# Gated cross-attention with a routed expert layer on one core: weight quarters, values and scores in another order

## The chip, the cores and the metric

The kernel runs on one core of one Trainium2 chip. The metric is device time in microseconds of one execution. Engines are called TensorE (PE), VectorE (DVE), ScalarE (ACT), GpSimd (POOL) and SyncE (SP); "queue" is an engine's stream of instructions, in which it also issues its transfers.

## The reference

Eight batches of 256 rows and 512 columns. Attention runs over the columns, with 16 heads of 16 channels; then every row is a token of a layer with 12 experts, of which it takes two.

```python
# x, ctx: (8, 256, 512);  Wq..Wo: (256, 256);  w1, w3: (12, 320, 512);  w2: (12, 512, 320)
h = layernorm(x)
q, k, v = Wq @ h + bq, Wk @ ctx + bk, Wv @ ctx + bv        # (256, 512) per batch, 16 heads x 16
p = softmax(q^T k / 4)                                     # (512, 512) per head
x = x + tanh(g0) * (Wo @ (p v) + bo)
h = layernorm(x)                                           # 2048 tokens of 512
w, i = top_k(softmax(h @ gate_w.T), 2);  w = w / sum(w)
x = x + tanh(g1) * sum over the two experts of w * ((silu(h @ w1.T) * (h @ w3.T)) @ w2.T)
```

## The kernel before

**Slots.** The attention runs as a pipeline of ten slots (`slots`, L351). In slot t, phase a projects batch t to K, Q and V, phase b makes scores, exponents and values of batch t-1, phase c normalises and projects the values of batch t-2 and makes its second layer norm and gate logits; p loads and normalises x and ctx of batch t+1. Slot 0 has only a and p, slot 1 has a, b and p, slot 8 has b and c, slot 9 only c. Slots 2 to 5 are a hardware loop of two rounds, the others are written out.

**Steps.** Each slot has 16 steps v (VS). In step v TensorE (L1327 to L1343) makes the first score group of step v+1 (`scores`, L1202: two heads of one quarter of the keys, into one of two PSUM tensors S), then the extra work that `EXTRA` (L322) lists for the step (k0, k1, q0, q1, v0 to v3 are projections into bank MA; o0, o1, t0, t1, lg are output projection, turning of the normed tokens and gate logits, in bank MC), then the second score group, then the values of step v (`values`, L1241). A score group waits until the exponent two groups earlier is made, since S has two tensors. ScalarE makes 32 exponents a slot (L724), two a step, of 1024 columns each. VectorE evicts MA, MC and O in the same order; every fourth step it copies O, the values and (in 16 rows of each 32) the sums of exponents, to `osum` (L982).

**Splits.** The experts' products are made with f16 high and low parts. The parts are made in 48 quarters of 512 KB in the shadow of the attention: ScalarE loads a quarter into one of three buffers wf (`load_quarter`, L697), VectorE writes high and low half to one of two buffers wp (`split_quarter`, L815: L823, L825), which first waits until the store of the quarter two before has landed, and ScalarE stores them (`store_quarter`, L702) and issues the load three quarters on. It does this in its own order, at the end of the exponents of the step two after the split, and waits there for the low half. `quarters` (L335) gives the steps: 4 quarters in slot 1, 6 in each of slots 2 to 7, 8 in slot 8. The experts' weights are read back after the last store.

**SyncE's order in a slot** (L435): loads for batch t+1; then for phase c a transfer of the sums (L461), their inverses to DRAM (L466), eight moves of 16 rows from `osum` to `oc` (L470), eight broadcasts of inverse sums to `zc` (L477); then for phase a the parts of K and Q go to DRAM in three copies each and are read back stacked (L482, L485); then the stores of x and of the normed tokens. Each waits where it stands, and what is behind it waits too.

**Phase c on VectorE.** At step ON_AT = 5 it multiplies `oc` by `zc` (L904) into `on` and casts to `os` (L906); GpSimd makes the low half (L580). LN_AT, XN_AT, XN2_AT and CS_AT are the steps of the layer norm's statistics, the norm, the second norm and the cast of the context.

**Experts.** After the attention the tokens are ranked and 43 tiles of 128 rows are gathered and run (`tiles`, L388).

A second version of the attention (`guard`) is there for inputs whose sums leave a range; it does not run here.

## Time and profile before

| | |
|---|---|
| median of 3 runs | 817.38 us (808.57 to 820.51) |
| profiled execution | 816.6 us, span 814.9 us |
| granted TensorE clock, mean | 0.88 |
| busy: TensorE / VectorE / ScalarE / GpSimd | 663.1 / 430.0 / 325.1 / 239.7 us |
| 16 DMA engines, mean over the span | 191 GB/s |

The granted clock is given as a share of 2.4 GHz; its other level is 1.2 GHz. Times in the rows count from the span's start. "[2.86 <-DVE V L931]" says that the engine stood idle for 2.86 us before the instruction, and that the V of line 931 on VectorE ended it. A row with "x4" is four instructions of one kind merged, with their time from first to last. "SPq" and "ACTq" are transfers issued by those queues; their time is that of the issue.

### The profile page before, as it was taken

The page shows a single profiled execution, that of the slowest core. Times are in us where ns is not written, and L with a number is a line of the kernel's source. Part 1 is how long each engine was busy: PE and PEld are TensorE (multiplying, and loading weights), DVE is VectorE, ACT ScalarE, POOL GpSimd, SP SyncE. Part 2 cuts the span into 40 slices and gives each one's busy share as a digit, 9 for nine tenths or more (in the row PEclk, how much of TensorE's full clock was granted, in tenths as well). Part 3 has the DMA queues.
Part 4 walks back from the last instruction along what each step waited for, and adds up shares of the span by engine and source line. Part 5 has one row for each costly group of instructions (what it writes and reads, how often), then busy time and mean ns, then how long its engine had stood idle before and what let it go on. Part 6 is the DMA issues. An engine that isn't in the chain of part 4 may idle for free.

```text
span 814.9 us, 14231 instructions
## 1 busy us (share of the span) xinstructions
PE 663.1 (81%) x4335; PEld 303.2 (37%) x4336; DVE 430.0 (53%) x761; ACT 325.1 (40%) x391; POOL 239.7 (29%) x184
## 2 busy tenths in 40 slices
PE   5878976977979879879876825059999999999993
PEld 3712222312222223232221113046666666666661
DVE  5536667585794785665646743753333333333330
ACT  0047855745646556546555610002222222222221
POOL 4032223222331331322111102233354433454422
PEclk8879989998997989879888865569999999999998
DMA  8447877768787887857767537524677787664533
GB/s 249 139 129 241 258 247 247 220 224 277 199 276 200 254 267 215 265 163 200 244 208 207 182 106 259 205 81 92 169 185 212 230 222 205 182 116 91 84 47 39
DMA packets 68470, 155.56 MB, mean 191 GB/s; under 512 B 9733, under 2 KB 15366, under 8 KB 66886
## 3 DMA queue, kind: packets, MB, share of 16 engines
q1 hardware_dynamic: 36368, 76.56, 29.8%
q10 hardware_dynamic: 22422, 55.87, 21.0%
q0 software_dynamic: 9632, 22.55, 14.6%
q8 instruction: 22, 0.36, 0.2%
q14 instruction: 26, 0.21, 0.1%
HBM read 92.04 MB, written 58.46 MB: 185 GB/s over the span
## 4 chain that ended last, share of the span: by engine, by line
PE 49%; DVE 15%; DMA 12%; issue 9%; SPq 8%; POOL 2%; ACT 2%; ACTq 2%; DVEq 0%; POOLq 0%
PE S L1393 15%; PE O L1414 9%; PE O L1253 7%; DMA ocz<-inverse_sums 5%; PE S L1214 5%; SPq L470 4%; DMA out<-yo,slot_out 3%; SPq L477 3%; DVE wp L825 3%; PE MC L1288 3%; PE MA L1288 2%; PE S L1380 2%; ACT prob L724 2%; PE MC L1308 2%; DVE wp L823 2%
## 5 line engine op out<-in xcount | busy, mean ns | idle before, releaser
L724 ACT ACTIVATE prob<-S 128x1024 f32<-128x1024 f32 x256 | 253.2, 1025 | 207.8 <-PE S L1214 144.0
L1253 PE MATMUL O<-prob,V 128*32 128x512 f32 x1024 | 156.0, 685 | 0.1
L1393 PE MATMUL S<-W,xT 128*128 x1032 | 149.9, 303 | 1.2 <-DVE xT L1158 1.2
L1214 PE MATMUL S<-Q,K 48*128 48x512 f16 x512 | 107.9, 428 | 52.2 <-ACT prob L724 46.0
L1393 PEld LDWEIGHTS S<-W,xT 128*128 128x128 f16 x1032 | 100.2, 99 | 39.0 <-issue 1.4
L1214 PEld LDWEIGHTS S<-Q,K 48*128 48x128 f16 x512 | 24.4, 94 | 216.9 <-ACT prob L724 149.7
L652 POOL DMA_INDIRECT out<-yo,slot_out x43 | 69.0, 1604 | 119.8 <-ACT yo L769 71.7
L1414 PE MATMUL O<-W,hT 128*128 (+1 forms) x344 | 90.3, 381 | 1.0 <-DVE hT L1178 1.0
L1166 DVE SCALAR_TENSOR_TENSOR hh<-S,act 128x320 f32<-128x320 f32 x43 | 21.1, 492 | 126.9 <-PE S L1393 124.2
L825 DVE SCALAR_TENSOR_TENSOR wp<-wf,wp 128x1024 f16<-128x1024 f32 x48 | 82.4, 1716 | 1.7
L628 POOL DMA_INDIRECT xg<-tokens_normed,slot_tok x43 | 42.6, 990 | 44.7 <-PE S L1380 32.5
L769 ACT ACTIVATE yo<-O,slot_w 128x512 f32<-128x512 f32 x43 | 29.6, 688 | 60.7 <-PE O L1414 56.4
L763 ACT ACTIVATE hs<-hh 128x320 f16<-128x320 f32 x43 | 20.2, 470 | 78.2 <-DVE hh L1166 78.2
L756 ACT ACTIVATE act<-S 128x320 f32<-128x320 f32 x43 | 18.8, 437 | 79.3 <-PE S L1393 75.8
L1414 PEld LDWEIGHTS O<-W,hT 128*128 128x128 f16 (+1 forms) x344 | 31.6, 97 | 49.4 <-issue 29.1
L1270 PE MATMUL MA<-w4s,cs 128*128 128x256 f16 x192 | 29.7, 296 | 22.4 <-DVE V L931 20.3
L823 DVE TENSOR_SCALAR wp<-wf 128x1024 f16<-128x1024 f32 x48 | 47.7, 993 | 0.1
L580 POOL TENSOR_TENSOR ks<-kf,ks 128x1024 f16<-128x1024 f32 x7 | 14.9, 2134 | 110.8 <-DVE ks L924 110.8
L580 POOL TENSOR_TENSOR os<-kf,os 128x1024 f16<-128x1024 f32 x8 | 17.4, 2171 | 94.5 <-DVE os L906 94.5
L1288 PE MATMUL MC<-os,w4s 128*128 128x512 f16 x96 | 32.9, 477 | 14.3 <-DVE os L906 12.1
L982 DVE COPY osum<-O 128x512 f32<-128x512 f32 x32 | 22.0, 687 | 40.5 <-PE O L1253 40.5
L1178 DVE COPY hT<-S 128x640 f16<-128x640 f16 x43 | 21.2, 492 | 41.3 <-PE S L1404 40.3
(152 smaller groups left out, 670.7 us busy)
## 6 DMA issues: line engine op xcount, KB each, us to landing
wf<-wall ACTq DMA_DIRECT2D x48, 512.0 KB, 6.7
weight_parts<-wp ACTq DMA_DIRECT2D x48, 512.0 KB, 4.7
W<-weight_parts SPq DMA_DIRECT2D x10, 2048.0 KB, 9.7
K<-k_parts SPq DMA_DIRECT2D x8, 1024.0 KB, 6.7
Q<-q_parts SPq DMA_DIRECT2D x8, 1024.0 KB, 6.7
k_parts<-ks SPq DMA_DIRECT2D x24, 256.0 KB
q_parts<-qs SPq DMA_DIRECT2D x24, 256.0 KB
ctx<-ctx_in SPq DMA_DIRECT2D x8, 512.0 KB, 6.0
```

What stands on the lines that cost most here:

```text
L470: sp.dma_start(oc[dst0:dst0 + DK, :, :], src).then_inc(g.oz, 16)
L580: pool.tensor_tensor(parts[:, 1], f[:, :, :], parts[:, 0], ALU.subtract).then_inc(lo, 1)
L628: pool.indirect_dma_start(out=xg[j % TR][:, :], out_offset=None, in_=xn_dram[:, :], in_offset=bass.IndirectOffsetOnAxis(ap=slot_tok[:, j:j ...
L652: pool.indirect_dma_start(out=out[:, :], out_offset=bass.IndirectOffsetOnAxis(ap=slot_out[:, j:j + 1], axis=0), in_=yo[j % TR][:, :], in_o ...
L724: act.activation(prob[:, u % RING, :], S[u % 2][:, :], ACT.Exp, scale=SCALE).then_inc(g.exp, 1)
L823: dve.tensor_scalar(c[:, 0], w[:, :], WS, None, ALU.mult).then_inc(s_whi, 1)
L825: dve.scalar_tensor_tensor(out=c[:, 1], in0=w[:, :], scalar=WS, in1=c[:, 0], op0=ALU.mult, op1=ALU.subtract).then_inc(s_wlo, 1)
L1214: last = pe.matmul(S[u % 2][:, s * T:(s + 1) * T], K[par][r0:r0 + rows_, 2 * g4 + n, st * P:(st + 1) * P], Q[par][r0:r0 + rows_, 2 * g4 + ...
L1253: last = pe.matmul(O[g4 % 2][2 * DK * j:2 * DK * (j + 1), :], V[par][:, st, head(g4, j), :], prob[:, u % RING, (j % 2) * T:(j % 2 + 1) * T ...
L1288: last = pe.matmul(bank[:, :], w4s[:, wp_, w, k, m * P:(m + 1) * P], src[:, xp, k, :], start=(n == 0), stop=(n == 3 * CT - 1))
L1393: last = pe.matmul(ps, xT[par][:, xp * TT + k, :], W[:, bass.ds(off + (w * WCOL + (2 * k + n) * F), F)], start=(k == 0 and (xp, w) == (0, 0)),
L1414: last = pe.matmul(y_ps[:, :], hT[par][0:rows_, block, :], W[0:rows_, bass.ds(off + (w * WCOL + W2 + k * T), T)], start=(n == 0), stop=(n ...
```

## The change

- Weights: four quarters in each of slots 2 to 7 (steps 2, 6, 9, 12), four at the end of slot 0, eight in slots 1 and 8, two in slot 9, two in the first two expert tiles. Four buffers wf instead of three. SyncE stores the quarters, in places of its own order between the transfers of K and Q; ScalarE only issues the load four quarters on, at the exponents of the step three after the split. In slot 0 it does so ahead of its first exponent. The read of the last expert's weights waits for the last stores, the others do not.
- Values: `osum` holds the groups in another order, so that four moves bring the second half of the values over the rows that held the sums, once these are read. The multiply reads `osum` itself. The inverse sums come in one broadcast. The rows of Wo are laid out to match. The low half of the normed values is made by VectorE, not GpSimd. `xn2` shares its memory with `xn`, with waits for that.
- SyncE's order: phase c's transfers and K's writes come first, then the loads for batch t+1.
- Scores: both score groups of step v+1 come ahead of the step's extra work. o0 and o1 move to steps 8 and 9 (o1 no longer in two halves), t0, t1, lg to 13, 14, 15.

```diff
-    WFS = 3
+    WFS = 4
-    z_dram = nc.dram_tensor("inverse_sums", [GH, GROUPS, T], F32).ap()
+    z_dram = nc.dram_tensor("inverse_sums", [GH, 2, CT * T], F32).ap()
-        xn2 = sb("xn2", [P, CT, T], F32, att)
+        xn2 = xn
-        EXTRA = {0: "k0", 1: "k1", 2: "q0", 3: "q1", 4: "v0", 5: "v1", 6: "v2", 7: "o0", 8: "o1a", 9: "o1b",
-                 10: "v3", 12: "t0", 13: "t1", 14: "lg"}
-        ON_AT, LN_AT, XN_AT, XN2_AT, CS_AT, SPLIT_AT = 5, 6, 8, 10, 11, 3
-        OZ = 16 * 4 * GH
+        EXTRA = {0: "k0", 1: "k1", 2: "q0", 3: "q1", 4: "v0", 5: "v1", 6: "v2", 8: "o0", 9: "o1",
+                 10: "v3", 13: "t0", 14: "t1", 15: "lg"}
+        ON_AT, LN_AT, XN_AT, XN2_AT, CS_AT, SPLIT_AT = 5, 7, 8, 11, 12, 3
+        OZ = 16 * (GH + 1)
@@ quarters
-            if t.i is None and t.add in (0, B + 1):
-                return []
-            if t.i is None and t.add == 1:
-                steps, first = (4, 7, 10, 13), At(None, 0, 0)
+            if t.i is None and t.add == 0:
+                steps, first = (15, 15, 15, 15), At(None, 0, 0)
+            elif t.i is None and t.add == 1:
+                steps, first = (1, 3, 5, 7, 9, 11, 13, 14), At(None, 0, 4)
             elif t.i is None and t.add == B:
-                steps, first = (0, 2, 4, 6, 8, 10, 12, 13), At(None, 0, QUARTERS - 8)
+                steps, first = (0, 2, 4, 6, 8, 10, 12, 13), At(None, 0, QUARTERS - 12)
+            elif t.i is None and t.add == B + 1:
+                steps, first = (7, 7), At(None, 0, QUARTERS - 4)
             else:
-                steps = (0, 2, 5, 8, 10, 13)
-                first = At(t.i, 12, 4 + 6 * (t.add - 2)) if t.i is not None else At(None, 0, 4 + 6 * (t.add - 2))
+                steps, first = (2, 6, 9, 12), At(t.i, 4 * t.mul, 4 * t.add + 4)
@@ SyncE, one slot
+                    def over_sums(j):
+                        r0 = 2 * DK * j
+                        sp.dma_start(osum[par][r0 + DK:r0 + 2 * DK, 0:CT, :], osum[par][r0:r0 + DK, CT:2 * CT, :])\
+                            .then_inc(g.oz, 16)
+                    if c:
+                        bc = t.before(2)
+                        wait(sp, g.os, bc, GROUPS, GROUPS, s_bog)
+                        wait(sp, g.on, bc, 1, 1)
+                        sp.dma_start(zl[:, :], osum[par][DK::2 * DK, :, :]).then_inc(g.zl, 16)
+                        wait(sp, g.rz, bc, 1, 1)
+                        sp.dma_start(z_dram.rearrange("j h n -> (j h n)").rearrange("(p n) -> p n", p=P), zr[:, :]).then_inc(g.zst, 16)
+                        for j in range(GH):
+                            over_sums(j)
+                    if a:
+                        wait(sp, g.qk, t, KQ_READS, 0, s_bog)
+                        wait(sp, g.kh, t, 1, 1)
+                        write(k_dram, ks, 0, (0, 1), g.kst)
+                    if c:
+                        wait(sp, g.zst, bc, 16, 16)
+                        sp.dma_start(zc.rearrange("p m t -> p (m t)"),
+                                     z_dram.rearrange("j h n -> (j h) n").unsqueeze(1)
+                                     .to_broadcast([2 * GH, DK, CT * T])).then_inc(g.oz, 16)
+                    if a:
+                        wait(sp, g.kl, t, 1, 1)
+                        write(k_dram, ks, 1, (2,), g.kst)
                     if p:
...
                         load_ctx(nxt)
                         load_x(nxt)
...
                     if a:
+                        weights(0, 3)
                         wait(sp, g.qh, t, 1, 1, s_bog)
                         write(q_dram, qs, 0, (0, 2), g.qst)
...
                         read(K, k_dram)
                         wait(sp, g.ql, t, 1, 1, s_bog)
                         write(q_dram, qs, 1, (1,), g.qst)
                         wait(sp, g.qst, t, KQ_WRITES, KQ_WRITES, s_bog)
                         read(Q, q_dram)
+                        weights(3, 10)
+                    else:
+                        weights(0, 9)
...
+                    weights(10 if a else 9, VS)
@@ ScalarE
-            def store_quarter(q):
-                c = q.add % 4
-                wait(act, s_wlo, q, 1, 1, s_bias)
-                act.dma_start(w_dram[bass.ds(over(q, 4).value(), 1), :, :, c * WQ:(c + 1) * WQ]
-                              .rearrange("e p h n -> p (e h) n"), wp[q.add % 2][:, :, :]).then_inc(s_wst[q.add % 2], 16)
+            def load_behind(q):
                 if q.i is not None or q.add + WFS < QUARTERS:
+                    wait(act, s_wlo, q, 1, 1, s_bias)
                     load_quarter(q.before(-WFS))
...
                     if not b_:
+                        if a and not guard:
+                            for n in range(WFS):
+                                load_quarter(At(None, 0, n))
+                        for _, q in splits:
+                            load_behind(q)
                         return
...
-                            if u == 2 * min(v + 2, VS - 1) + 1:
-                                store_quarter(q)
+                            if u == 2 * min(v + 3, VS - 1) + 1:
+                                load_behind(q)
@@ VectorE
-                            dve.tensor_tensor(on[:, :, :], oc[:, :, :], zc[:, :, :], ALU.mult).then_inc(g.on, 1)
+                            dve.tensor_tensor(on[:, :, :], osum[par][:, 0:CT, :], zc[:, :, :], ALU.mult)\
+                                .then_inc(g.on, 1)
                             wait(dve, g.on, bc, 1, 2)
                             dve.tensor_copy(os_[:, 0], on[:, :, :]).then_inc(g.oh, 1)
+                            low(bc, os_, on, g.oh, g.ol)
...
-                            dve.tensor_copy(osum[1 - par][:, g4, :], O[g4 % 2][:, :]).then_inc(g.os, 1)
+                            at = g4 % 2 * CT + g4 // 2
+                            dve.tensor_copy(osum[1 - par][:, at, :], O[g4 % 2][:, :]).then_inc(g.os, 1)
@@ TensorE
                     for v in range(VS):
                         if b_ and v + 1 < VS:
-                            scores(bb, 1 - par, v + 1, (0,))
+                            scores(bb, 1 - par, v + 1)
                         what = EXTRA.get(v, "")
...
-                        if b_ and v + 1 < VS:
-                            scores(bb, 1 - par, v + 1, (1,))
```

## Rows read from the trace of the kernel before

**Rows 1.** windows by slot: stretch, length, busy us per engine, clock, DMA share, GB/s

```profile
46.10:90.10 44.00, 40.18 (x244) 10.18 (x242) 20.95 (x30) 32.69 (x34) 9.56 (x7) 0.89 0.65 209
...
90.10:146.90 56.80, 45.37 (x279) 13.94 (x278) 39.04 (x55) 31.74 (x33) 15.42 (x10) 0.91 0.76 239
...
257.30:312.40 55.10, 47.31 (x277) 14.12 (x278) 38.08 (x54) 31.65 (x32) 15.39 (x10) 0.87 0.77 243
...
424.90:473.90 49.00, 37.40 (x224) 9.15 (x220) 30.52 (x39) 29.08 (x30) 5.94 (x4) 0.86 0.58 183
...
473.90:515.00 41.10, 11.99 (x38) 6.72 (x38) 15.29 (x74) 0.56 (x2) 5.17 (x4) 0.53 0.50 164
...
542.00:815.00 273.00, 257.72 (x1927) 163.18 (x1927) 89.28 (x214) 68.59 (x129) 107.40 (x82) 0.98 0.60 142
```

**Rows 2.** timeline of slot 5, first half: start, us, engine, operation, [idle]

```profile
261.97 0.35 SPq L466 DMA_DIRECT2D inverse_sums<-zr  x1
...
265.90 4.03 SPq L477 DMA_DIRECT2D ocz<-inverse_sums  x8
...
270.11 1.97 SPq L482 DMA_DIRECT2D k_parts<-ks  x3
...
274.92 1.23 DVE L904 TENSOR_TENSOR kf<-ocz 128x1024 f32<-128x1024 f32 x1 [4.10 <-DMA ocz<-inverse_sums]
...
277.26 0.83 PE L1270 MATMUL MA<-w4s,cs 128*128 128x256 f16 x6 [2.86 <-DVE V L931]
```

**Rows 3.** timeline of slot 5, second half, same columns

```profile
292.75 0.39 PE L1214 MATMUL S<-Q,K 48*128 48x512 f16 x2 [1.58 <-ACT prob L724]
...
295.76 3.02 DVE L825 SCALAR_TENSOR_TENSOR wp<-wf,wp 128x1024 f16<-128x1024 f32 x1
...
299.01 0.56 ACTq L706 DMA_DIRECT2D weight_parts<-wp  x1
...
301.63 0.39 PE L1214 MATMUL S<-Q,K 48*128 48x512 f16 x2 [2.82 <-ACT prob L724]
```

**Rows 4.** page, part 5: groups of instructions, busy us and mean ns, idle before

```profile
L724 ACT ACTIVATE prob<-S 128x1024 f32<-128x1024 f32 x256 | 253.2, 1025 | 207.8 <-PE S L1214 144.0
...
L1166 DVE SCALAR_TENSOR_TENSOR hh<-S,act 128x320 f32<-128x320 f32 x43 | 21.1, 492 | 126.9 <-PE S L1393 124.2
...
L825 DVE SCALAR_TENSOR_TENSOR wp<-wf,wp 128x1024 f16<-128x1024 f32 x48 | 82.4, 1716 | 1.7
...
L823 DVE TENSOR_SCALAR wp<-wf 128x1024 f16<-128x1024 f32 x48 | 47.7, 993 | 0.1
```

**Rows 5.** page, part 6: issues of the context's load, KB each, us to landing

```profile
ctx<-ctx_in SPq DMA_DIRECT2D x8, 512.0 KB, 6.0
```

**Rows 6.** timeline, end of slot 0

```profile
41.50 2.50 DVE L848 CAST cs<-ctx 128x1024 f16<-128x1024 f32 x1
...
46.08 2.85 ACT L724 ACTIVATE prob<-S 128x1024 f32<-128x1024 f32 x3 [34.34 <-PE S L1214]
```

**Rows 7.** stores of the weights, line 706: issue to landing

```profile
DMA to landing us min/median/max: 3.1/4.7/8.8
```

**Rows 8.** timeline of slot 1: SyncE's queue and ScalarE

```profile
64.92 1.15 SPq L482 DMA_DIRECT2D q_parts<-qs  x1
...
75.40 0.37 SPq L485 DMA_DIRECT2D Q<-q_parts  x1
...
75.48 2.85 ACT L724 ACTIVATE prob<-S 128x1024 f32<-128x1024 f32 x3 [1.67 <-PE O L1253]
```

**Rows 9.** reads of Q: issue to landing

```profile
DMA to landing us min/median/max: 5.4/6.7/10.0
```

**Rows 10.** timeline, last slot

```profile
481.07 3.85 SPq L477 DMA_DIRECT2D ocz<-inverse_sums  x8
...
486.83 1.23 DVE L904 TENSOR_TENSOR kf<-ocz 128x1024 f32<-128x1024 f32 x1 [4.54 <-issue]
```

**Rows 11.** windows of slot 5, its last stretch

```profile
303.00:312.40 9.40, 9.40 (x54) 3.09 (x54) 3.11 (x5) 5.41 (x6) 0.00 (x0) 0.69 0.76 254
```

90 lines of the change are left out of this document (44 added, 46 removed).

## The prediction

> **What bounds the kernel now.** I cut the span into stages first [rows 1], by the starts of the slots. Slot 1 takes 44.0 us, slots 2 to 7 together 334.8 us (from 90.1 to 424.9, so 55.8 each), slot 8 takes 49.0, the last slot and what follows it 41.1, and the expert tiles 273.0. In the tiles TensorE is busy for 257.7 of 273 us at a granted clock of 0.98; the change hardly touches them. So the question is the slots.
>
> Take slot 5 as the pattern, in the third row of [rows 1]: 55.10 us, TensorE busy 47.31 at a mean granted clock of 0.87. 47.31 x 0.87 = 41.2 us is the work at full clock, 6.1 us is what the lower clock costs, and 55.10 - 47.31 = 7.8 us TensorE stands idle. ScalarE is busy 31.7, VectorE 38.1. No engine but TensorE is near the slot's length, so a slot can fall only by the idle time and by the clock that is lost behind it.
>
> The timeline names the idle pieces. First, step 5: VectorE waits 4.10 us for the last of the inverse sums, the values' multiply comes at 274.92, the eviction of the values' projection is queued behind it, and TensorE stands 2.86 us [rows 2]. Its next products run on the low clock. Second and third, [rows 3]: ScalarE holds its queue until a quarter's low half is written, then issues a store and a load; TensorE waits 1.58 and then 2.82 us for the exponent behind it. The low half before the longer wait took 3.02 us, against a mean of 1.72 [rows 4]: it lies beside GpSimd's own subtraction of the same kind of tile. The three make 7.26 of the 7.8 us; the rest, 0.5, I count to the second wait.
>
> **The change, part by part.** The sum is made against the profiled execution, 816.6 us, which is 0.8 below the median of the runs.
>
> *Fewer quarters in slots 2 to 7, stores on SyncE, load waits a step later.* Two of six splits go from each slot. A split is 0.99 + 1.72 = 2.7 us of VectorE [rows 4], 5.4 us a slot. ScalarE now waits at the steps' ends 3 behind the split instead of 2, and issues one transfer instead of two (0.56 us for the store by [rows 3]; I take 0.6 for each). The waits of 2.1 and 2.82 us go: 4.9 us a slot. What is late next is VectorE itself in steps 9 to 13: residual and statistics, a split, the second layer norm, copy of sums, context cast, another split that lies beside GpSimd's subtractions (up to 3.7), and only then the eviction of the first turned tile, for which TensorE waits before it turns the second. Counting these from the rows' durations gives about 11.3 us from the end of "o1" to that eviction, where TensorE needs some 10. I put 2.0 us of new idle there, between 0 and 4.
>
> *Values moved in place, inverse sums in one broadcast.* Before, SyncE issued four moves, the store of the inverse sums at 261.97, four more moves and, from 265.90, 8 broadcasts (4.03), the last of which let VectorE go at 274.92; the writes of K stood behind them until 270.11 [rows 2]. Now 4 moves come behind the store of the inverse sums, two K writes (0.66 each, from 1.97 for three) and one broadcast of 512 KB. Counted from the slot's start at 257.3: the store at +4.7 [rows 2], moves until +8 (the last four took about 3.5 before the first broadcast), K writes until +9.5, the broadcast issued by +10. A 512 KB load of this queue lands after 6.0 us [rows 5], so at +16 against +17.6 now; with the moves and K writes ahead of it on the queue up to +18. Against this, the low half of the values moves from GpSimd to VectorE, ahead of the eviction that TensorE waits for: as long as the multiply of the same size, 1.23 us [rows 2]. So the 2.86 us become about 2.0 (between 0 and 6). GpSimd's 2.1 us are free, which costs nothing: it had slack (15.4 busy of 55.1).
>
> *Both score groups first.* In the projection steps TensorE runs without a gap in either order, so nothing. In other steps it helps ScalarE a little; below 0.5 us a slot, taken as 0. It may also cost: the projection now stands behind the second group, which needs the exponent before. It is covered while ScalarE (two exponents of 1.03 a step [rows 4]) is ahead of TensorE, which it is once its waits are gone.
>
> Slots 2 to 7: idle 7.8 becomes 2.0 + 2.0 = 4.0, so -3.8; with less of it, the clock's loss of 6.1 falls perhaps by its share to 4.3, so -1.8. Together -5.6 a slot, **-33.6** for six. Ends: no gain, and -9 a slot (all idle but 1 us gone and half of the clock's loss).
>
> *Slot 0, four splits at its end.* This costs. There are two buffers of split quarters, so the third split waits until the first store landed and the fourth for the second. SyncE issues these only after the read of Q. VectorE is free at 44.0 (41.50 + 2.50, [rows 6]). Split one lies beside GpSimd's subtraction for the context: 3.0 for the low half as in [rows 3] and 0.7 for the high one, to 47.7. Split two is undisturbed, 0.7 + 1.23 as the multiply of [rows 2], so 1.95 with what lies between, to 49.7. Store one is issued at 47.8 and lands 4.7 us later [rows 7], 52.5; split three to 54.5; store two landed by then; split four to 56.5. ScalarE has all four waits for them in its queue ahead of the first exponent, and issues a load (0.6). So the first exponent starts near 57 instead of 46.08 [rows 6]: **+11**. With landings of 3.1 us it is +9, with 8.8 us +15 [rows 7]. Nothing covers it: TensorE's scores of the batch were there when ScalarE began, and both engines had been waiting.
>
> *Slot 1, eight splits instead of four.* The store of the split at step 3 stands in SyncE's order behind the read of Q. That read was issued 29.3 us after the first exponent (75.40 against 46.08), since the write of Q's low half, issued at 64.92 behind the 1 MB read of K, took 10.5 us [rows 8]. The read of Q lands after 5.4 to 10.0 us [rows 9], the store behind it, say 8 us after its issue: +37.5. Only then can VectorE make the split of step 7, whose end, +39.5, is what ScalarE's queue waits for after its 22nd exponent; it had done that one at +31 [rows 8], and would now at +33. That is 6 to 7 us. Four more splits, each waiting for a store of 4.7 us two before it, add some 3 at the slot's end: **+10**, between +2 and +14.
>
> Here a rule speaks against my term, after the row: the 10.5 us show transfers of one queue staying behind each other. The Trainium skill (DMA: Bandwidth & Descriptors, "Issuing engines are not separate DMA queues") says that transfers of all issuing engines run on the same 16 engines and interleave, and that issuing from several saves only issue time. By that the store would take its 4.7 us wherever it is issued, slot 1's term would be about +6 and the whole 4 us less. The trace does not show a store behind a 1 MB read on one queue, so it leaves this open; the issue order behind SyncE's wait would stay in either case.
>
> *Slot 8.* No projections; the broadcast follows the moves at once, about 4 us earlier, and ScalarE's store issues go. But the split of step 13 waits for the store of step 10, which stands behind the tokens' store, perhaps 3 us. 49.0 becomes 46: **-3** (-7 to +1).
>
> *Last slot.* The eight broadcasts from 481.07 took 3.85 us and the multiply came at 486.83 [rows 10]; one issue and 5 to 6 us of landing make that 1 us earlier (0 to 2). The low half saves 0.9 more. Two splits at step 7 (1.95 each, with GpSimd idle) stand ahead of the first residual and cost 2. **0** (-2 to +3). The last two splits lie in the gap of 124.2 / 42 = 2.96 us in which VectorE waits in each tile [rows 4]: **+0.5** (0 to 2).
>
> Sum: 11 + 10 - 33.6 - 3 + 0 + 0.5 = -15.1; 816.6 - 15.1 = 801.5, so 802.
>
> **The rivals.** *Slots fall further.* With no wait at the turned tiles and the broadcast landing at +15, TensorE would hold its clock: -8.5 a slot, -51, with the start at +19: 778 to 785. For it: GpSimd and ScalarE have slack (15.4 and 31.7 busy of 55.1 [rows 1]). Against it: VectorE's chain in steps 9 to 13 is as long as TensorE's. Chance 0.25.
>
> *Half the gain.* The chain through steps 9 to 13 costs 4 us and the clock gives nothing back: -3 a slot, -18; start +21: about 817, no change. For it: the clock was at 0.69 from 303.0 to 312.4, though TensorE was busy for all of that stretch [rows 11]. Chance 0.2.
>
> *Slower: the broadcast is late.* It stands behind moves and K writes on one queue and is one transfer, not eight in flight. If it lands at +20 instead of +17.6, the multiply, and 1.23 us of the low half on top, hold the projection at step 6 for 2.86 + 2.4 + 1.2 = 6.5 us. With 2.0 at the turned tiles that is 8.5 of idle, as much as before; the slots gain nothing, and the start's 21 less slot 8's 3 stand: 835. It decides from a landing at about +20 on. For it: 5.0 us passed between the end of the eight issues and the multiply [rows 2]. Against: 4 moves and 7 issues are gone from ahead of it. Chance 0.1.
>
> *The change does not do what it says* in one part: reordering the scores. It moves no number above.
>
> **How the numbers follow.** My forecast, 790 to 813, has 0.45. A difference under 2% (801 to 834) is about what a measurement of this kernel cannot tell from none. The forecast's half below 801 (0.21) and the first rival (0.25) are faster: 0.46. The other half (0.24) and the second rival (0.2) are the same: 0.44. Slower: 0.10. The range, 779 to 827, leaves out the far end of the first rival and the slower one.
>
> **What would show it.** First exponent near 57 us (right: 55 to 61). In slot 1, one stall of ScalarE of 5 to 9 us before its 23rd exponent. Slots 2 to 7 at 50 us, with splits in four steps, no ScalarE idle over 3 us, TensorE's largest idle at step 6 and at the second turned tile. The multiply 16 to 18 us into the slot. If the first exponent starts before 50, or slots stay above 54, the forecast is wrong.

## The result and the profile after

The change makes the kernel slower: 844.14 us (843.04 to 845.38, 4 runs) against 814.65 (4 runs of the kernel before), ratio 1.036, 95% interval 1.028 to 1.045. The profiled execution has a span of 842.9 us at a mean granted clock of 0.861, against 814.9 and 0.880: 28.0 us to explain. By 2% the verdict is "slower", where I forecast 802.

Windows by slot answer to [rows 1]: stretch, length, busy us per engine, clock, DMA share, GB/s. The second row is slots 2 to 7 together, the third slot 5, the fourth slot 8.

```profile
58.60:119.40 60.80, 40.35 (x240) 9.57 (x240) 31.23 (x38) 30.54 (x32) 10.21 (x6) 0.81 0.67 214
119.40:446.50 327.10, 274.93 (x1658) 86.14 (x1658) 196.76 (x293) 186.19 (x194) 80.17 (x50) 0.86 0.65 202
288.20:343.90 55.70, 46.80 (x278) 15.08 (x280) 33.83 (x51) 31.60 (x33) 14.33 (x9) 0.84 0.63 194
446.50:499.20 52.70, 36.28 (x224) 10.69 (x222) 29.62 (x40) 28.98 (x31) 3.06 (x3) 0.88 0.69 197
```

The same window over slots 2 to 7 of the kernel before:

```profile
89.90:424.80 334.90, 279.96 (x1658) 85.40 (x1659) 224.01 (x311) 191.61 (x193) 86.87 (x56) 0.88 0.75 233
```

So slots 2 to 7 are 7.8 us shorter (7.7 between the copies of sums that end them), not 33.6. Length is idle time plus busy time, and busy time times clock is the work: before, per slot, 9.2 idle, 41.1 work and 5.6 lost to the clock; after, 8.7 idle, 39.4 work and 6.4 lost to the clock (the clock is rounded to 0.01, so each of the last two terms is good to 0.2 us a slot). TensorE waits nearly as long as before and runs no faster. The work fell by 1.7 us though the number of products is the same; the run f3 below shows that the order of the products alone moves time between "busy" and "idle", so the two terms are compared with care between kernels of different order. Slot 1 is 60.8 against 43.9, slot 8 52.7 against 49.2, and the first exponent comes 12.5 us later.

Slot 5, first half, answers to [rows 2]; columns are start, us, engine, operation, count, and in brackets the idle time before it with its releaser:

```profile
292.13 0.36 SPq L484 DMA_DIRECT2D inverse_sums<-zr  x1
292.52 2.53 SPq L466 DMA_DIRECT2D osum<-osum  x4
295.39 1.35 SPq L471 DMA_DIRECT2D k_parts<-ks  x2
296.85 0.63 SPq L496 DMA_DIRECT2D ocz<-inverse_sums  x1
...
306.18 1.23 DVE L938 TENSOR_TENSOR kf<-osum,ocz 128x1024 f32<-128x1024 f32 x1 [3.78 <-DMA ocz<-inverse_sums]
...
309.31 0.42 DVE L967 SCALAR_TENSOR_TENSOR V<-MA,bv_all 128x256 f32<-128x256 f32 x1
...
309.79 1.46 PE L1313 MATMUL MA<-w4s,cs 128*128 128x256 f16 x6 [4.01 <-DVE V L967]
```

Counted from the copy of sums that ends the slot before (288.22 here, 256.81 in the kernel before), the one broadcast is issued at +8.6, where the eight had begun at +9.1. The multiply comes 9.33 us after that issue, against 9.02 before, so at +18.0 against +18.1; then the low half and the eviction, and TensorE has stood 4.01 us where it had stood 2.86.

Slot 5, second half, answers to [rows 3]:

```profile
327.81 2.24 DVE L880 CAST cs<-ctx 128x1024 f16<-128x1024 f32 x1
329.98 0.68 DVE L855 TENSOR_SCALAR wp<-wf 128x1024 f16<-128x1024 f32 x1
330.69 3.03 DVE L857 SCALAR_TENSOR_TENSOR wp<-wf,wp 128x1024 f16<-128x1024 f32 x1
333.64 0.68 DVE L987 COPY xT<-MC 128x512 f32<-128x512 f32 x1
...
334.45 1.11 PE L1347 MATMUL MC<-ident,xn 128*128 128x128 f32 x4 [3.71 <-DVE xT L987]
...
337.36 3.59 PE L1351 MATMUL MC<-gate,xT 128*128 128x12 f32 x16
...
341.53 1.94 ACT L747 ACTIVATE prob<-S 128x1024 f32<-128x1024 f32 x2 [8.95 <-PE S L1257]
```

VectorE takes the context's cast (2.24) and the split (0.68 + 3.03) ahead of the first turned tile's copy at 333.64. TensorE waits 3.71 for it. Then the gate's product takes 3.59 us, and ScalarE has nothing to do for 8.95 us, since the scores for it stand behind that product. The two waits of [rows 3] on ScalarE's store are gone; this one took their place.

The waits of TensorE over slots 2 to 7 (total us, times, longest), first of the changed kernel, then of the kernel before:

```profile
PE MA L1313 <- DVE V L967: 25.4, 6, 4.9
PE MC L1347 <- DVE xT L987: 19.4, 6, 3.7
PE S L1257 <- ACT prob L747: 9.9, 11, 5.0
```

```profile
PE S L1214 <- ACT prob L724: 34.5, 17, 4.4
PE MA L1270 <- DVE V L931: 20.3, 6, 4.6
```

The wait for exponents fell by 24.6 us, the wait at step 6 grew by 5.1, and 19.4 us for the turned tile are new. The changed kernel's lines of groups and of DMA issues that bear on the rest:

```profile
L747 ACT ACTIVATE prob<-S 128x1024 f32<-128x1024 f32 x256 | 245.7, 1023 | 229.3 <-PE S L1257 158.4
...
L855 DVE TENSOR_SCALAR wp<-wf 128x1024 f16<-128x1024 f32 x48 | 37.8, 787 | 38.1 <-DMA weight_parts<-wp 37.8
...
weight_parts<-wp SPq DMA_DIRECT2D x46, 512.0 KB, 6.9
...
ctx<-ctx_in SPq DMA_DIRECT2D x8, 512.0 KB, 10.4
```

The start, answering to [rows 6] and [rows 8], and slot 8:

```profile
44.58 3.02 DVE L857 SCALAR_TENSOR_TENSOR wp<-wf,wp 128x1024 f16<-128x1024 f32 x1
...
47.63 11.09 SPq L427 DMA_DIRECT2D weight_parts<-wp  x4
...
53.67 0.69 DVE L855 TENSOR_SCALAR wp<-wf 128x1024 f16<-128x1024 f32 x1 [4.21 <-DMA weight_parts<-wp]
...
58.57 1.94 ACT L747 ACTIVATE prob<-S 128x1024 f32<-128x1024 f32 x2 [46.62 <-DVE wp L857]
...
93.22 0.37 SPq L474 DMA_DIRECT2D Q<-q_parts  x1
...
100.67 0.69 DVE L855 TENSOR_SCALAR wp<-wf 128x1024 f16<-128x1024 f32 x1 [12.17 <-DMA weight_parts<-wp]
...
103.09 3.77 ACT L747 ACTIVATE prob<-S 128x1024 f32<-128x1024 f32 x4 [11.50 <-DVE wp L857]
...
454.56 0.64 SPq L496 DMA_DIRECT2D ocz<-inverse_sums  x1
455.25 17.27 SPq L427 DMA_DIRECT2D weight_parts<-wp  x4
...
465.03 0.69 DVE L855 TENSOR_SCALAR wp<-wf 128x1024 f16<-128x1024 f32 x1 [10.03 <-DMA weight_parts<-wp]
...
466.90 1.22 DVE L938 TENSOR_TENSOR kf<-osum,ocz 128x1024 f32<-128x1024 f32 x1
```

The first exponent waits for four splits. In slot 1 SyncE reads Q at 93.22; the store behind it lets VectorE go at 100.67 after 12.17 us, and ScalarE, which waits for that split, stands 11.50 us. In slot 8 the store is issued at 455.25, right behind the broadcast, and VectorE waits 10.03 us for it. The multiply stands behind that split in VectorE's order; by slot 5's 9.33 us from issue to multiply the inverse sums would be there at 463.9, three microseconds before it starts; that is an estimate, since in slot 8 of e5 below the same span was 10.25. Of the 37.8 us that VectorE waits for stores, 22.7 lie in slots 0 and 1, 15.1 behind slot 7, and none between.

### The profile page after: what moved, and what is told of

Its sections match the earlier page's. It is cut to its first block, busy times and chain, and to the rows that moved or that the text cites. A ratio compares the mean times of both kernels' runs of the same rounds, so it can differ in the third digit from the quotient of the medians.

```text
span 842.9 us, 14098 instructions
## 1 busy us (share of the span) xinstructions
PE 657.0 (78%) x4335; PEld 305.1 (36%) x4336; DVE 429.9 (51%) x769; ACT 317.6 (38%) x391; POOL 229.0 (27%) x176
## 4 chain that ended last, share of the span: by engine, by line
PE 46%; DMA 20%; DVE 16%; issue 9%; POOL 3%; SPq 2%; PEldq 1%; ACT 1%; POOLq 0%; DVEq 0%; ACTq 0%
PE S L1434 15%; PE O L1455 8%; DMA weight_parts<-wp 6%; DMA ocz<-inverse_sums 6%; PE O L1296 6%; PE MA L1331 4%; DMA out<-yo,slot_out 3%; PE MC L1351 3%; PE S L1257 3%; DMA q_parts<-qs 3%; DVE wp L857 2%; PE MC L1331 2%; PE S L1421 2%; DVE wp L855 2%; POOL rstd L612 1%
## 5 line engine op out<-in xcount | busy, mean ns | idle before, releaser
L747 ACT ACTIVATE prob<-S 128x1024 f32<-128x1024 f32 x256 | 245.7, 1023 | 229.3 <-PE S L1257 158.4
L1257 PE MATMUL S<-Q,K 48*128 48x512 f16 x512 | 92.9, 422 | 51.6 <-ACT prob L747 43.7
L1434 PEld LDWEIGHTS S<-W,xT 128*128 128x128 f16 x1032 | 99.9, 98 | 38.5 <-issue 1.4
L1257 PEld LDWEIGHTS S<-Q,K 48*128 48x128 f16 x512 | 19.8, 95 | 180.4 <-ACT prob L747 150.8
L857 DVE SCALAR_TENSOR_TENSOR wp<-wf,wp 128x1024 f16<-128x1024 f32 x48 | 73.2, 1526 | 1.7
L610 POOL TENSOR_SCALAR veps<-mv 128x2 f32<-128x2 f32 x16 | 6.2, 385 | 197.7 <-DVE mv L997 101.6
L855 DVE TENSOR_SCALAR wp<-wf 128x1024 f16<-128x1024 f32 x48 | 37.8, 787 | 38.1 <-DMA weight_parts<-wp 37.8
L652 POOL DMA_INDIRECT xg<-tokens_normed,slot_tok x43 | 42.4, 987 | 42.6 <-PE S L1421 30.1
L1296 PEld LDWEIGHTS O<-prob,V 128*32 128x32 f32 x1024 | 21.1, 113 | 46.6 <-issue 34.2
L1331 PE MATMUL MC<-os,w4s 128*128 128x512 f16 x96 | 27.3, 427 | 13.6 <-DVE os L941 10.7
## 6 DMA issues: line engine op xcount, KB each, us to landing
ctx<-ctx_in SPq DMA_DIRECT2D x8, 512.0 KB, 10.4
```

What stands on the lines that cost most here:

```text
L652: pool.indirect_dma_start(out=xg[j % TR][:, :], out_offset=None, in_=xn_dram[:, :], in_offset=bass.IndirectOffsetOnAxis(ap=slot_tok[:, j:j ...
L747: act.activation(prob[:, u % RING, :], S[u % 2][:, :], ACT.Exp, scale=SCALE).then_inc(g.exp, 1)
L855: dve.tensor_scalar(c[:, 0], w[:, :], WS, None, ALU.mult).then_inc(s_whi, 1)
L857: dve.scalar_tensor_tensor(out=c[:, 1], in0=w[:, :], scalar=WS, in1=c[:, 0], op0=ALU.mult, op1=ALU.subtract).then_inc(s_wlo, 1)
L1257: last = pe.matmul(S[u % 2][:, s * T:(s + 1) * T], K[par][r0:r0 + rows_, 2 * g4 + n, st * P:(st + 1) * P], Q[par][r0:r0 + rows_, 2 * g4 + ...
L1296: last = pe.matmul(O[g4 % 2][2 * DK * j:2 * DK * (j + 1), :], V[par][:, st, head(g4, j), :], prob[:, u % RING, (j % 2) * T:(j % 2 + 1) * T ...
```

## The experiments

They are told by question. The edits are shown shortened: words in angle brackets stand for code that is left out, and so are semaphore counts that go with an edit. This table has the profiled execution of each, in us: the first exponent, the length of slot 1, of slots 2 to 7 together, of slot 8, and of all behind it. A slot ends where its fourth copy of sums starts, as in the windows above. Each length is of one execution: the profiled ones lie up to 9.5 us from the median of their kernel (g2 847.48 against 838.00, e1 828.60 against 835.48, f4 779.87 against 786.38), and stretches that an edit doesn't touch differ by up to 4 us. So a difference of a few microseconds in a stretch says nothing by itself. Ratios are to runs of the kernel before on the same chip, with a 95% interval.

| kernel | first exp. | slot 1 | 2 to 7 | slot 8 | rest | ratio |
|---|---|---|---|---|---|---|
| before | 46.1 | 43.9 | 334.8 | 49.2 | 341.0 | 1 |
| after | 58.6 | 60.8 | 327.1 | 52.7 | 343.7 | 1.036 [1.028, 1.045] |
| i1 split at 14 | 58.8 | 60.8 | 295.1 | 55.2 | 342.8 | 0.991 [0.988, 0.994] |
| e5 ScalarE stores | 59.2 | 48.8 | 327.8 | 42.9 | 343.4 | 0.999 [0.995, 1.003] |
| e1 eight pieces | 58.9 | 60.8 | 311.5 | 54.1 | 341.1 | 1.020 [1.010, 1.029] |
| e3 multiply at 7 | 59.9 | 60.9 | 318.6 | 53.6 | 342.8 | 1.027 [1.020, 1.034] |
| e4 old quarters | 46.4 | 48.8 | 359.2 | 52.2 | 340.2 | 1.035 [1.027, 1.044] |
| g2 store first | 60.1 | 55.3 | 331.3 | 55.5 | 343.3 | 1.024 [1.015, 1.032] |
| g3 two halves | 60.4 | 47.6 | 322.6 | 42.4 | 340.9 | 1.002 [0.998, 1.006] |
| f1 next scores | 60.8 | 48.4 | 318.9 | 41.9 | 343.8 | 1.007 [0.997, 1.016] |
| f3 order alone | 48.3 | 43.9 | 333.3 | 52.4 | 340.5 | 1.012 [1.000, 1.024] |
| f2 e5 + e1 | 60.0 | 49.2 | 303.1 | 43.3 | 341.4 | 0.987 [0.978, 0.995] |
| h1 f2 + multiply at 7 | 59.3 | 49.2 | 306.7 | 43.8 | 342.7 | 0.983 [0.976, 0.990] |
| h2 f2 + split at 14 | 59.7 | 47.8 | 283.6 | 45.9 | 342.4 | 0.956 [0.949, 0.962] |
| h3 f2 + next scores | 59.9 | 47.6 | 305.9 | 42.4 | 341.5 | 0.984 [0.976, 0.993] |
| f4 f2 + all three | 60.1 | 47.7 | 287.2 | 41.7 | 341.4 | 0.967 [0.956, 0.979] |
| g1 f4, two splits first | 51.8 | 47.7 | 288.2 | 41.5 | 343.2 | 0.954 [0.946, 0.962] |
| h4 g1, SyncE stores | 50.7 | 62.1 | 286.5 | 56.5 | 345.4 | 0.977 [0.969, 0.984] |
| g5 g1, later loads | 46.6 | 48.7 | 290.3 | 42.6 | 342.7 | 0.950 [0.942, 0.958] |
| i2 | 47.8 | 50.0 | 283.5 | 42.2 | 343.9 | 0.938 [0.933, 0.944] |

My theories after the result: (A) the stores in SyncE's queue cost the start, slot 8 and perhaps the slots; (B) the single broadcast is slow; (C) the order of the last steps costs the slots. Rival to each: what it costs is covered, or moves elsewhere.

### Where the stores are issued

**e5, the stores on ScalarE again,** all else as changed:

```diff
-    (SyncE) for v, q in splits: if v0 <= v < v1: store_quarter(q)
+    (ScalarE, load_behind) wait(act, s_wlo, q, 1, 1, s_bias); act.dma_start(<store of q>)
```

> The changed kernel with its own schedule of quarters, but each store issued by ScalarE ahead of the load behind it, none by SyncE. Theory A: the stores' place in SyncE's order, behind the read of Q, is what holds VectorE for 12.2 us in slot 1, and the queue's order behind the broadcast what holds it for 10.0 in slot 8: both waits fall below 4 us, slot 0 stays as it is (first exponent near 58), slots 2 to 7 keep their length within 1.5 us; total 818 to 830. Rival B: stores are slow wherever they are issued: slot 1 stays above 56 us, total within 5 us of 844.

822.80 us; 1.036 becomes 0.999. Slot 1 falls by 12.0 us and slot 8 by 9.8, slots 2 to 7 do not move. The stores land 4.4 us after their issue instead of 6.9. So the place of the stores costs the two slots in which a split follows closely on a store, and there alone.

**g2, in slot 1 the store of step 3's quarter ahead of the wait for Q's parts and the read of Q:**

```diff
+    if t.i is None and t.add == 1: weights(3, 5)
     wait(sp, g.qst, t, KQ_WRITES, KQ_WRITES, s_bog); read(Q, q_dram)
-    weights(3, 10)
+    weights(5 if t.i is None and t.add == 1 else 3, 10)
```

> The changed kernel with, in slot 1 alone, the store of step 3's quarter ahead of SyncE's wait for Q's low half and the read of Q. Theory A (the predicted one): it is SyncE's order, the store standing behind that wait, that holds VectorE for 12.2 us at step 7; the wait falls under 4 us and slot 1 from 60.8 to 48 to 53 us, total 8 to 12 us less. Rival B: the transfers of one queue stay behind each other in any case, so the store and with it Q land as late: slot 1 stays above 57.

838.00 us. Slot 1 is 55.3, between the 60.8 of the change and the 48.8 of e5. VectorE's wait at this split:

```profile
94.90 0.69 DVE L857 TENSOR_SCALAR wp<-wf 128x1024 f16<-128x1024 f32 x1 [4.92 <-DMA weight_parts<-wp]
```

against 12.17. So the order behind Q's read is worth some 5.5 of slot 1's 12 us. The trace of the changed kernel agrees: of the 12.17 us, from 88.50 on, 5.1 had passed when SyncE issued the first store behind Q's read at 93.64, and 7.0 lie between that issue and the landing. What is left in g2 are waits for later stores, 2.73, 2.96 and 2.03 us, which still stand in SyncE's order. Slot 8 is untouched by this edit and did not gain (55.5).

**h4, the kernel g1 (below) with the stores by SyncE:**

```diff
-    (ScalarE, load_behind) act.dma_start(<store of q>)
+    (SyncE) for v, q in splits: if v0 <= v < v1: store_quarter(q)
```

> The kernel of g1 (two splits in slot 0, eight-piece broadcast, multiply at step 7, split at step 14, next scores first), with the stores issued by SyncE again in place of ScalarE. If SyncE's queue is the cause by itself, slot 1 is over 55 us (47.7), slot 8 over 50 (41.5), and the ratio is 0.97 to 0.99 (g1: 0.954). Rival: it was slow only through the broadcast in the same queue: slot 8 under 44, ratio under 0.96.

801.98 us. The first theory holds on both slots (62.1 and 56.5), though the broadcast here is eight pieces: stores issued by SyncE, with their place in its order, cost 14.4 + 15.0 us, and slots 2 to 7 nothing (286.5 against 288.2). In slot 8 of it:

```profile
418.76 0.69 DVE L856 TENSOR_SCALAR wp<-wf 128x1024 f16<-128x1024 f32 x1 [9.13 <-DMA weight_parts<-wp]
```

The store that it waits for was issued at 412.69, behind the eight pieces: 3.1 us of this wait lie before the issue and 6.1 behind it.

**e4, quarters, steps and counts of splits as before,** six a slot and none in slot 0, all else as changed:

```diff
-    steps, first = (2, 6, 9, 12), At(t.i, 4 * t.mul, 4 * t.add + 4)
+    steps, first = (0, 2, 5, 8, 10, 13), At(t.i, 12, 4 + 6 * (t.add - 2))   # and four, not eight, in slot 1
```

> The changed kernel with the quarters at the steps of the kernel before (none in slot 0, 4 in slot 1, 6 in slots 2 to 7, 8 in slot 8), stores still by SyncE, four load buffers. Theory A: slots 0 and 1 end near 92 us instead of 119.4, since no split waits for a store there; slots 2 to 7 grow by 1 to 3 us each for two more splits: total 822 to 835. Rival B: the start costs nothing that the other slots don't give back, and the order of SyncE's queue with more stores in it is the cause: 840 or more.

848.92 us, as slow as the change, but elsewhere: the first exponent is back at 46.4 and slot 1 at 48.8, while slots 2 to 7 take 359.2. The multiply comes 19.4 to 23.1 us into a slot. Six splits a slot, with all else as changed, take 24.4 us more over these slots than before the change; whether by the stores, the broadcast or the steps, this run doesn't separate. It shows that the longer start alone is not the cause of the loss, and that fewer splits a slot were a part of the change that helped.

### The broadcast

**e1, the broadcast in eight pieces,** as before the change but with values in place:

```diff
-    sp.dma_start(zc, z_dram.rearrange("j h n -> (j h) n").unsqueeze(1).to_broadcast([2 * GH, DK, CT * T]))
+    for r in range(2 * GH):
+        sp.dma_start(zc[DK * r:DK * (r + 1)], z_dram[r // 2, r % 2:r % 2 + 1, :].to_broadcast([DK, CT * T]))
```

> The changed kernel with its one broadcast of inverse sums (512 KB) issued as eight of 64 KB, all else equal. Theory A: the single broadcast is slow by itself and holds what stands behind it on SyncE's queue (9.3 us to the multiply in slot 5, 7.0 in the last slot where nothing competes, and VectorE's 10.0 us wait for a store in slot 8). Then the multiply of the last slot comes about 6 us after the first broadcast's issue instead of 7, in slots 2 to 7 it comes 15 to 16.5 us after the slot's start instead of 18, slot 8's wait falls to about 5 us, and the total falls by 8 to 18 us, to 826 to 836. Rival B: the queue is late because of the weights' stores that now stand in it; then the multiply stays within 1 us of where it was, and the total within 5 us of 844.

835.48 us, 1.036 becomes 1.020. In the profiled execution the slots gain 15.6 us; it was the fastest of four, and the ratios give some 14 us for the whole kernel. Its slot 5 begins at 278 us; the eight issues and the multiply:

```profile
286.50 4.61 SPq L497 DMA_DIRECT2D ocz<-inverse_sums  x8
...
293.41 1.23 DVE L939 TENSOR_TENSOR kf<-osum,ocz 128x1024 f32<-128x1024 f32 x1 [1.36 <-DMA ocz<-inverse_sums]
```

6.91 us from the first issue to the multiply instead of 9.33, though the issues alone take 4.61. The single broadcast saves SyncE 4 us of issuing and costs 2.4 us where it counts. Before the change eight pieces took 9.02 us [rows 2]: eight moves were ahead of them, four of them issued right before, where now there are four moves in all. That this is the reason isn't shown.

**f2, the edits of e1 and e5 together:**

> The kernel with the stores by ScalarE, and the broadcast of inverse sums in eight pieces. Theory A: the broadcast is slow by itself, so its 14 us add to the stores' 30: 0.978 to 0.988 of before, the multiply 15 to 17 us into the slots. Rival B: the broadcast was slow only since it shared a queue with the stores: 0.995 to 1.003.

801.64 us, faster than before the change (0.987). With the stores on ScalarE the eight pieces are worth 24.7 us over the slots (327.8 to 303.1).

**g3, e5 with the broadcast in two halves of columns,** each from the same eight rows:

```diff
-    sp.dma_start(zc, <all columns>)
+    for m in range(CT): sp.dma_start(zc[:, m, :], <columns m * T to (m + 1) * T>)
```

> The kernel with the stores by ScalarE, and the broadcast as two transfers, each of all 128 rows and half the columns. In the last slot the single one needed 7.0 us from issue to multiply at no more than 185 GB/s, where the eight pieces reached up to 287. Theory A: the eight source rows as the outermost dimension keep the transfer to half of the DMA engines; two halves have the same eight rows and so stay at 185 GB/s and 7 us, and the total stays within 4 us of the run with one. Rival B: one transfer is slow because it is one; two overlap, the multiply comes 1 us or more earlier and the total falls by 8 us or more, as with eight.

816.23 us, 1.002, as e5 within the intervals. The slots have 5.2 us less. In the last slot the multiply comes 6.06 us after the first issue; for the one broadcast it was 6.95 (505.93 to 512.88) and for the eight before it 5.76 [rows 10]. So the number of transfers may help a little. Windows of one microsecond in the last slot, of the changed kernel and then of e1, show how the two ways move:

```profile
508.60:509.60 1.00, 0.00 (x0) 0.00 (x0) 0.00 (x0) 0.00 (x0) 0.00 (x0) 0.50 0.52 131
509.60:510.60 1.00, 0.00 (x0) 0.00 (x0) 0.00 (x0) 0.00 (x0) 0.00 (x0) 0.50 0.54 131
```

```profile
495.00:496.00 1.00, 0.00 (x0) 0.00 (x0) 0.00 (x0) 0.00 (x0) 0.00 (x0) 0.50 0.62 131
496.00:497.00 1.00, 0.00 (x0) 0.00 (x0) 0.00 (x0) 0.00 (x0) 0.00 (x0) 0.50 0.74 127
```

The single broadcast keeps about half of the DMA engines' time busy, as the expectation's first theory had it, but it moves as many bytes as the eight pieces, 131 GB/s; the 185 and 287 GB/s that the expectation names don't show in these windows. So why one broadcast of 512 KB is slower than eight of 64 KB is not settled: no run changed the number of source rows.

**e3, the multiply at step 7 instead of 5:**

```diff
-        ON_AT, LN_AT, XN_AT, XN2_AT, CS_AT, SPLIT_AT = 5, 7, 8, 11, 12, 3
+        ON_AT, LN_AT, XN_AT, XN2_AT, CS_AT, SPLIT_AT = 7, 7, 8, 11, 12, 3
```

> The changed kernel with the multiply by the inverse sums at step 7 instead of 5, all else equal, so that no eviction of a values' projection stands behind the wait for the broadcast. Theory A: TensorE's 4.2 us a slot of waiting at step 6, and the low clock behind it, are a loss of their own: slots 2 to 7 fall by 4 to 5 us each, the total to 815 to 822. Rival B: what is gained at step 6 is lost again at the turned tiles in steps 13 to 14, where VectorE is late anyway: less than 10 us in total, 835 or more.

842.52 us, as the changed kernel within the intervals (1.027 against 1.036). Its profiled execution, the fastest of four, has 8.5 us less in the slots. The wait at step 6 is gone, but the wait for the turned tile grew from 19.4 to 37.1 us over the six slots: the time saved at step 6 went largely there, as the rival had it.

**h1, the same edit on f2:**

> The kernel with the eight-piece broadcast and the stores on ScalarE (slots 2 to 7: 303.1 us), with the values' multiply issued in step 7 in place of step 5. If the wait at the multiply still costs there, it gives 1.5 to 3 us a slot, sum 285 to 294. Rival: the broadcast in eight pieces lands in time and the multiply in step 5 costs nothing; then the later multiply only makes the copies behind it later: sum 300 or more.

804.67 us, slots 306.7: the rival holds. Once the multiply comes at +15.4 to +16.9, as in slots 3 to 7 of f2, there is no more to gain here.

### The last steps of a slot

**f4, f2 with three edits,** the multiply at step 7, the fourth split at step 14, and the next slot's scores ahead of the logits:

```diff
-    ON_AT = 5;  steps = (2, 6, 9, 12)
+    ON_AT = 7;  steps = (2, 6, 9, 14)
+    if b_ and v == VS - 1 and not last_b and not guard: scores(t, par, 0)   # ahead of EXTRA
     what = EXTRA.get(v, "")
```

> All mends together: stores by ScalarE, broadcast in eight pieces, multiply at step 7, next batch's scores ahead of the logits, and the split of step 12 at step 14, behind the evictions of the turned tiles. Theory A: each wait is its own loss, so they add: slots 2 to 7 near 47 to 49 us, 0.935 to 0.955 of before, with slots 0 and 1 still at 105 to 110 us. Rival B: VectorE's chain of steps 9 to 14 takes over: slots above 51 us, 0.965 or more.

786.38 us, slots 287.2. What f2 left in the slots is in one of the three; h1, h2 and h3 take them one by one.

**h2, f2 with the fourth split at step 14:**

```diff
-                steps, first = (2, 6, 9, 12), At(t.i, 4 * t.mul, 4 * t.add + 4)
+                steps, first = (2, 6, 9, 14), At(t.i, 4 * t.mul, 4 * t.add + 4)
```

> The same kernel with only the fourth split moved from step 12 to step 14, behind the turned tiles' copies. If the split holds those copies up (the wait of PE for xT), it gives 1 to 3 us a slot, sum 285 to 297, and the xT wait of 3.7 us a slot falls under 1.5. Rival: the wait only moves to the logits: sum 301 or more.

781.63 us, slots 283.6, a little below the 285 to 297 of the first theory: the whole gain of f4 by one number, 19.5 us of f2's slots or 3.3 a slot. The wait for the turned tile is 1.4 us in all instead of 16.4.

**h3, f2 with the last of f4's edits alone,** the next slot's scores ahead of the logits:

> The same kernel with only the next slot's scores issued ahead of the logits at the end of a slot. With the stores still as they were this gave 8.9 us over six slots (327.8 to 318.9). If the terms add: sum 294. Rival: it hides the same idle time that the earlier broadcast already took: sum 300 or more.

804.40 us, slots 305.9: nothing; the rival holds. **f1**, the same edit on e5:

> The kernel with the stores by ScalarE (the fourth experiment), and in step 15 the next batch's first scores ahead of the gate logits instead of behind them. Theory A: since the logits were moved to the last step, which has no score group of its own ahead of them, ScalarE stands 7.9 us there in each slot (323 to 331 us of slot 5), and TensorE's low clock makes it dear; with the scores first slots 2 to 7 fall by 2 to 3.5 us each, the total to 0.97 to 0.985 of before. Rival B: TensorE is the bound at the slot's end, whatever the order: the sum of slots 2 to 7 stays within 4 us of 327.8 and the total at 0.995 to 1.003.

816.93 us. Here the slots of the profiled execution fell by 8.9 us, but the ratio is 1.007, against 0.999 for e5 in another set of runs: the timed runs show no gain of this edit.

**i1, the split at step 14 as the only edit of the changed kernel:**

> The changed kernel with one number altered: the fourth split in step 14 in place of 12. If the split ahead of the turned tiles' copies is a loss of its own, slots 2 to 7 fall from 327.1 us by 12 to 20 us, to 307 to 315, and the ratio from 1.036 to about 1.015. Rival: while the stores and the single broadcast are late, the time only moves to the wait at step 6: sum 320 or more.

812.08 us: 1.036 becomes 0.991, and slots 2 to 7 fall by 32.0 us to 295.1, more than either theory had. The other single edits of the changed kernel give 15.6 us at most in the slots. Its window over slots 2 to 7, then the copies of the turned tiles, the split behind them, the gate's product and ScalarE's wait in its slot 5:

```profile
119.50:414.60 295.10, 255.02 (x1658) 78.20 (x1658) 187.06 (x293) 185.70 (x194) 78.33 (x50) 0.93 0.71 221
```

```profile
311.93 0.68 DVE L987 COPY xT<-MC 128x512 f32<-128x512 f32 x1
...
314.32 1.96 PE L1351 MATMUL MC<-gate,xT 128*128 128x12 f32 x16
...
314.81 1.22 DVE L857 SCALAR_TENSOR_TENSOR wp<-wf,wp 128x1024 f16<-128x1024 f32 x1
...
316.82 3.77 ACT L747 ACTIVATE prob<-S 128x1024 f32<-128x1024 f32 x4 [2.30 <-PE S L1257]
```

The copy of the first turned tile follows the context's cast at once and TensorE doesn't wait. The split's low half, no longer beside GpSimd's subtraction (330.14 to 332.64 in the changed kernel's slot 5), takes 1.22 us instead of 3.03; the gate's product 1.96 instead of 3.59; ScalarE stands 2.30 instead of 8.95. By the windows the six slots have 12.1 us less idle time of TensorE (52.2 to 40.1), and the clock went from 0.86 to 0.93, worth the other 20 us (38.5 to 17.9 lost). The waits at step 6 are still there (29.2 us against 25.4).

### The order of scores, and the start

**f3, both score groups first, as the only edit of the kernel before:**

```diff
-                            scores(bb, 1 - par, v + 1, (0,))
+                            scores(bb, 1 - par, v + 1)
-                        if b_ and v + 1 < VS:
-                            scores(bb, 1 - par, v + 1, (1,))
```

> The kernel before with one part of the change alone: both score groups of the next step ahead of the step's extra work. All steps, queues and quarters as before. Theory A (as predicted): worth nothing by itself, 0.995 to 1.003 of before. Rival B: TensorE's extra work now waits for the exponent of the group before, which ScalarE delays by its waits for the splits: 1.005 to 1.02. Rival C: ScalarE gets its scores earlier and idles less: 0.975 to 0.99.

820.18 us, 1.012 with an interval from 1.000 to 1.024: inconclusive. The slots differ by 1.5 us. Their split into terms moves all the same:

```profile
92.20:425.50 333.30, 267.79 (x1658) 80.96 (x1656) 224.34 (x310) 183.43 (x193) 86.81 (x56) 0.91 0.76 234
```

TensorE is busy for 12.2 us less than before the change and idle for 10.6 more, at a clock of 0.91 instead of 0.88. So idle time in two kernels of different order isn't the same quantity; i1 and the changed kernel, which differ in one step number, have the same order of products.

**g1, f4 with two splits in slot 0** instead of four, and four instead of two in the last slot:

```diff
-    steps = (15, 15, 15, 15)   # slot 0        (7, 7)         # last slot
+    steps = (15, 15)           # slot 0        (4, 4, 7, 7)   # last slot
```

> The mended kernel of the run before, with two splits at the end of slot 0 instead of four and four in the last slot instead of two (two of them ahead of the multiply). Theory A: the third and fourth split's waits for a landed store are what holds the first exponent; it moves from 60.1 to 50 to 52, and the total falls by 8 us, to 0.95 to 0.962 of before. Rival B: what is gained at the first exponent is lost in slot 1, whose own splits wait then: 0.963 or more.

779.33 us; the first exponent is at 51.8 instead of 60.1. **g5** is g1 with the loads behind these two splits issued by ScalarE in slot 1, behind its fourth exponent:

```diff
+    if t.i is None and t.add == 1 and u == 3:
+        for _, q in quarters(At(None, 0, 0)): load_behind(q)
```

> As the first of this group (two splits in slot 0), and ScalarE's stores and loads for these two come behind its fourth exponent in slot 1 instead of ahead of the first. Theory A: first exponent back at 46 to 48 us and 3 to 5 us less than the first of this group: 0.945 to 0.957 of before. Rival B: VectorE, which is busy with the two splits until 50, holds slot 1 as long: within 2 us of the first of this group.

775.96 us; the first exponent is at 46.6, as before the change. By the first exponents, the third and fourth split, which wait for stores to land, cost 8.3 us here, and ScalarE's wait for the other two 5.2; of the latter the whole time shows little (0.954 and 0.950, with intervals that overlap).

**i2, the best version:** two splits in slot 0 with later loads, stores on ScalarE, eight pieces, split at step 14; the multiply at step 5 and the order of logits as in the change:

```diff
-    ON_AT = 7   # of g5, back to 5, and the next slot's scores back behind the logits
+    ON_AT = 5
```

> The best kernel so far (two splits in slot 0, its loads issued in slot 1, stores on ScalarE, broadcast in eight pieces, split in step 14) with the multiply back in step 5 and the next slot's scores back behind the logits. If those two edits do nothing, it is within 1% of 0.950. Rival: they help only once the split is out of the way: 0.96 or more.

767.56 us, ratio 0.938 [0.933, 0.944]: the fastest, 52 us under the 819.74 of the kernel before in the same set of runs. The two edits that it lacks against g5 (0.950) were not needed. Its slots 2 to 7, and the store's wait in slot 8 that was 10.03 us:

```profile
97.80:381.30 283.50, 247.29 (x1656) 76.69 (x1656) 186.06 (x294) 184.65 (x193) 78.35 (x50) 0.97 0.73 229
```

```profile
391.46 0.69 DVE L861 TENSOR_SCALAR wp<-wf 128x1024 f16<-128x1024 f32 x1 [1.02 <-DMA weight_parts<-wp]
```

## Why the prediction was wrong

Term by term, forecast against measured, in us of the profiled executions:

| term | forecast | measured |
|---|---|---|
| slot 0, first exponent | +11 (9 to 15) | +12.5 |
| slot 1 | +10 (2 to 14) | +16.9 |
| slots 2 to 7 | -33.6 | -7.7 |
| slot 8 | -3 (-7 to +1) | +3.5 |
| last slot and tiles | +0.5 | +2.7 |
| sum | -15.1 | +28.0 |

The mean slot of 2 to 7 took 54.5 us, above the 54 that I had named as the sign of a wrong forecast.

**The step that failed is "what is late next" in slots 2 to 7.** The gains were forecast from slot 5, with 7.8 us idle to become 4.0; the mean slot had 9.2 and kept 8.7. I named the place: the context's cast, "another split that lies beside GpSimd's subtractions (up to 3.7), and only then the eviction of the first turned tile", with 2.0 us of new idle (0 to 4). The idle came, at 3.2 a slot (19.4 in six). What I priced wrong is what it does. I let the clock's loss fall from 6.1 to 4.3 for less idle time. It did not fall: 5.6 before and 6.4 after over the mean slot, 6.1 and 7.5 in slot 5 (46.80 us at 0.84). Behind the wait come the values of a step, the gate's product and then the scores that ScalarE needs, all at the lower clock in this stretch (0.84 over slot 5; the gate's product 3.59 against 1.96), and ScalarE stood 9 us. i1 moves this one split and nothing else: 32.0 us, 5.3 a slot, about 2.0 of idle time and 3.4 of clock. The same edit on f2, where TensorE idles less already, gave 3.3 a slot (h2), so the price of the wait depends on what surrounds it. With it slots 2 to 7 are 39.7 us under the kernel before, so the gains that I counted were there to be had, and this wait ate them. In idle time alone other misses are as large: 4.2 a slot at step 6 where I had 2.0, and 1.7 for exponents where I had none (9.9 us in six slots, half of it one wait of 5.0 as slot 2 begins). The move of the logits from step 14 to 15 I had not costed; the runs don't undo it, but where the next scores no longer stand behind the logits (h3) the time is the same.

**The broadcast** was forecast to land at +16 and to leave 2.0 us of TensorE's idle time; it came at +18.0 and left 4.2. My six microseconds came from a 512 KB load of another shape [rows 5], which itself landed after 10.4 us in the changed kernel; this broadcast took 9.3, and +18 was my upper end. e1 puts up to 15.6 us over six slots on it, f2 against e5 24.7. Of the 4.2 us, the low half that moved from GpSimd to VectorE was forecast at 1.23; no run puts it back, so its share isn't shown. It is no full case of the rival "slower: the broadcast is late", which needed +20 and slots no shorter than before: with i1 the same broadcast leaves them 39.7 shorter.

**The stores.** Slot 1 was right in its mechanism, the store behind the read of Q, and too small in size: ScalarE stood 11.5 us where I had 6 to 7. I had left the read of Q at 29.3 us behind the first exponent; it was issued 34.65 behind it (93.22 against 58.57). Here I weighed a rule of the Trainium skill (DMA: Bandwidth & Descriptors, "Issuing engines are not separate DMA queues"), by which issuing from several engines saves only issue time. h4 against g1 decides: the same stores issued by SyncE cost 29.4 us in two slots, and the ratio goes from 0.954 to 0.977. Part of that is SyncE's order, which lets a store out late (5.1 us in slot 1). But in slot 8 the store that VectorE waits for was issued at 455.25, right behind the broadcast, and landed only at 465.03, where ScalarE's stores took 4.4 us (median, e5): it was slow after its issue too, behind what its own queue held. That fits what the Trainium skill says (DMA: Bandwidth & Descriptors, "Queues, rings and completion order"), that SyncE and ScalarE each have their own ring on each of the DMA engines and that descriptors are taken in ring order; my runs show the wait, not the rings. In slot 8 I looked for the store of step 13 behind the tokens' store and missed the earlier one: the slot's first two splits stand close together (VectorE is done with them before the broadcast is issued), the third needs the store of the first, and that store, right behind the broadcast, holds VectorE for 10.03 us, with the multiply behind it.

**Slot 0** was right, in place and size (first exponent at 58.6 where I had 57). The scores' order, which I put at 0, is undecided (f3: at most 2.4%). The rival nearest in size, 835, had another mechanism; that it came nearer than my forecast is luck.

## What to carry to other kernels

When a stall is removed, follow the engine that is late next through to the one that feeds the critical engine, and price the new wait with the clock it leaves behind, not with its idle time alone: here 2.0 us of idle time came with 3.4 us of clock. An edit of a schedule has many numbers; move each alone before judging the whole, since one step number (12 to 14) turned 3.6% slower into 0.9% faster. A transfer that another engine soon waits for shouldn't share a queue with large ones, however small its issue time.
